# Laying the query and key parts in DRAM by chunk of 512 tokens, and loading a unit's pieces one by one

## The reference

```
xn = layernorm(x)
q, k, v = per head (16 heads of 16 features): xn @ W + b
attention: softmax(causal(q @ k^T / 4)) @ v, heads joined, @ Wo + bo
experts: logits = xn @ Wr; the best 2 of 8 experts, softmax over the two logits
         per expert: (clip(silu(xn @ Wg), -7, 7) * (xn @ Wu)) @ Wd, weighted and added
out = x + attention + experts
```

## Time and profile before

| what | value |
|---|---|
| median of 3 runs | 438.08 us (437.95 to 439.42) |
| the profiled execution | 438.36 us, of which the span of the engines is 436.4 us |
| PE matmul busy | 412.3 us, 94% of the span |
| DVE busy | 332.0 us, 76% |
| ACT, POOL busy | 222.4 us, 196.5 us |
| mean DMA rate | 163 GB/s |

### The profile page before, as it was taken

One profiled execution on the slowest core, in us unless ns is written; L12 is line 12 of the kernel. 1 busy time (PEld: TensorE's weight loads), 2 busy tenths in 40 slices (PEclk: granted clock), 3 DMA queues, 4 the chain that ended last, 5 costly groups with the idle time before them and its releaser, 6 DMA issues.

```text
span 436.4 us, 8151 instructions
## 1 busy us (share of the span) xinstructions
PE 412.3 (94%) x2755; PEld 246.4 (56%) x2755; DVE 332.0 (76%) x1043; ACT 222.4 (51%) x511; POOL 196.5 (45%) x223
## 2 busy tenths in 40 slices
PE   8998979989999999999799999999999999999993
PEld 8585414655364465566547567565667476556332
DVE  6827999999989859775287866789396988881795
ACT  1563362334646566545164355456555445646970
POOL 5331266576064187256474265415655255313320
PEclk9999979999999999999899999999999999999996
DMA  7289896788067089235954239805595336110782
GB/s 228 82 218 194 289 200 211 226 285 282 3 160 174 1 252 279 75 110 170 214 168 156 103 110 249 248 24 182 164 235 178 136 101 194 24 26 6 236 271 72
DMA packets 40372, 71.33 MB, mean 163 GB/s; under 512 B 5893, under 2 KB 30598, under 8 KB 40332
## 3 DMA queue, kind: packets, MB, share of 16 engines
q0 software_dynamic: 9360, 39.99, 29.1%
q1 hardware_dynamic: 27132, 26.76, 25.0%
q10 hardware_dynamic: 3840, 4.08, 3.7%
HBM read 55.85 MB, written 15.60 MB: 164 GB/s over the span
## 4 chain that ended last, share of the span: by engine, by line
PE 68%; DVE 21%; DMA 4%; issue 4%; ACT 1%; POOL 1%; SPq 0%; ACTq 0%; DVEq 0%; POOLq 0%
PE psum L1293 14%; PE psum L1330 14%; PE psum L1254 11%; PE psum L1273 11%; PE psum L1339 8%; DVE psum L981 7%; DVE mxa L984 4%; PE psum L1209 3%; PE psum L1185 3%; PE psum L1312 3%; DMA bqk<-in_bqk 2%; PE psum L1320 2%; DMA xg<-xn_rows,token 2%; DVE resid L953 1%; DMA x<-in_x 1%
## 5 line engine op out<-in xcount | busy, mean ns | idle before, releaser
L894 ACT ACTIVATE probs<-psum 128x512 f32<-128x512 f32 (+1 forms) x320 | 151.1, 581 | 40.9 <-PE psum L1273 40.3
L981 DVE CUSTOM_DVE_ANT_0 psum<-psum,maskrow 128x128 f32<-128x128 f32 (+3 forms) x256 | 121.4, 506 | 14.3 <-PE psum L1254 14.0
L1254 PE MATMUL psum<-packk,packq 96*128 96x512 bf16 (+3 forms) x384 | 94.2, 328 | 3.3 <-DVE mxb L981 1.2
L1273 PE MATMUL psum<-packq,packk 99*128 99x512 bf16 (+3 forms) x384 | 91.0, 330 | 3.3 <-ACT probs L894 2.1
L984 DVE TENSOR_REDUCE mxa<-psum 128x1 f32<-128x512 f32 x128 | 87.7, 685 | 5.4 <-PE psum L1254 5.3
L1293 PE MATMUL psum<-probs,v 128*32 128x512 f32 (+3 forms) x768 | 75.7, 503 | 1.0 <-POOL probs L821 0.9
L1254 PEld LDWEIGHTS psum<-packk,packq 96*128 96x128 bf16 x384 | 35.1, 97 | 56.1 <-issue 15.9
L821 POOL TENSOR_SCALAR_AFFINE_SELECT probs<-probs 128x512 f32<-128x512 f32 (+1 forms) x48 | 41.2, 863 | 44.8 <-ACT probs L894 44.7
L1273 PEld LDWEIGHTS psum<-packq,packk 99*128 99x128 bf16 x384 | 33.4, 98 | 42.7 <-issue 10.5
L788 POOL DMA_INDIRECT xg<-xn_rows,token x39 | 37.7, 967 | 38.9 <-PE psum L1320 27.4
L806 POOL DMA_INDIRECT expert_rows<-wvr,slots x39 | 39.3, 1008 | 31.8 <-ACT wvr L914 17.2
(11 more groups left out here) (120 smaller groups left out, 457.8 us busy)
## 6 DMA issues: line engine op xcount, KB each, us to landing
qk_parts<-stage SPq DMA_DIRECT2D x24, 256.0 KB, 3.9
stage<-expert_rows SPq DMA_DIRECT2D x16, 256.0 KB, 4.1
packq<-qk_parts SPq DMA_DIRECT2D x16, 192.0 KB, 5.4
packk<-qk_parts SPq DMA_DIRECT2D x14, 192.0 KB, 5.8
x<-in_x SPq DMA_DIRECT2D x4, 512.0 KB, 6.2
packq<-qk_parts SPq DMA_DIRECT2D x16, 128.0 KB, 6.0
xn_rows<-probs ACTq DMA_DIRECT2D x4, 512.0 KB, 14.7
out<-x SPq DMA_DIRECT2D x16, 128.0 KB, 3.0
```

Of the source, the lines that this page charges most:

```text
L894: act.activation(probs[:, g % RING, h, 0:width], psum[:, bank, 0:width], ACT.Exp, scale=SCALE)\
L981: ins = dve.tensor_tensor_reduce(out=chunk, in0=chunk, in1=maskrow[:, BANK - width:], scale=1.0, scalar=NEG, op0=ALU.add, op1=ALU.max, acc ...
L1254: pe.matmul(psum[:, bank, 0:width], packq[0:MAXROW, u % SLOTS, i // HALF, h, P * (i % HALF):P * (i % HALF + 1)], packk[0:MAXROW, u % SLOTS ...
L1273: ins = pe.matmul(psum[:, bank, at:at + width], packk[0:KROWS, u % SLOTS, j // HALF, h, P * (j % HALF):P * (j % HALF + 1)], packq[0:KROWS, ...
```

## The change

The DRAM tensor of the parts gets another order of dimensions: the chunk of 512 tokens moves ahead of feature and head. The four heads of one feature and one chunk then lie in one run of 4 x 512 x 2 = 4096 bytes, where before each head had a run of 1024 bytes. The loads are written with the dimensions part, feature, and heads-with-tokens; before, part and feature were one dimension. In the new order of the tensor, the chunk dimension stands between part and feature.

From unit 3 on, each of the six pieces has its own release: piece number c x 3 + r waits for step 10(u - 2) - 1 + (3(c x 3 + r) // 2), which is that same first step and the steps 1, 3, 4, 6 and 7 after it. The planner is given the same condition, so it orders the loads anew. Units 0 to 2 wait for what they waited for before.

```diff
+LOAD_EVERY = 3
...
+def step_before_load(u, c, r):
+
+    return NS * (u - SLOTS + 1) - 1 + (c * len(RUNS) + r) * LOAD_EVERY // 2
...
     for u in range(UNITS):
         b, g = divmod(u, G)
         for c in range(2):
-            after = [("SP", ("store", 4 * b + 2 * (g // 2) + c))]
-            if u >= SLOTS:
-                after += [("PE", ("s", NS * (u - SLOTS + 1) - 1, UH - 1))]
             due = 8 + 10 * c if u == 0 else 60000 + c if u == 1 else nat_due(u, 0) - 30000 + c
             for r in range(len(RUNS)):
+                after = [("SP", ("store", 4 * b + 2 * (g // 2) + c))]
+                if u >= SLOTS:
+                    after += [("PE", ("s", step_before_load(u, c, r), UH - 1))]
...
-        qk_d = nc.dram_tensor("qk_parts", [2, 2, PARTS, HD, H // 2, N], BF16).ap()
+        qk_d = nc.dram_tensor("qk_parts", [2, 2, PARTS, N // BANK, HD, H // 2, BANK], BF16).ap()
...
-                    cols = slice(T * b + BANK * n, T * b + BANK * (n + 1))
-                    sp.dma_start(qk_d[:, grp, part, :, :, cols].rearrange("o d h t -> (d h) o t"),
+                    sp.dma_start(qk_d[:, grp, part, T // BANK * b + n, :, :, :].rearrange("o d h t -> (d h) o t"),
...
-                    wait_filled(sp, ("s", NS * (u - SLOTS + 1) - 1, UH - 1))
+                    wait_filled(sp, ("s", step_before_load(u, c, r), UH - 1))
...
-                    src = qk_d[op, grp, first[op]:first[op] + length, :, h0:h0 + UH, T * b + BANK * c:T * b + BANK * (c + 1)]
-                    sp.dma_start(pack[row:row + HD * length, u % SLOTS, c, :, :],
-                                 src.rearrange("r d h t -> (r d) h t")).then_inc(pack_in[u % SLOTS][c], 16)
+                    src = qk_d[op, grp, first[op]:first[op] + length, T // BANK * b + c, :, h0:h0 + UH, :]
+                    sp.dma_start(pack[row:row + HD * length, u % SLOTS, c, :, :].rearrange("p h t -> p (h t)"),
+                                 src.rearrange("r d h t -> r d (h t)")).then_inc(pack_in[u % SLOTS][c], 16)
...
-              act.dma_start(packk[row:row + HD * length, 0, c, :, :],
-                              qk_d[1, 0, first:first + length, :, 0:UH, BANK * c:BANK * (c + 1)].rearrange("r d h t -> (r d) h t"))\
+              act.dma_start(packk[row:row + HD * length, 0, c, :, :].rearrange("p h t -> p (h t)"),
+                              qk_d[1, 0, first:first + length, c, :, 0:UH, :].rearrange("r d h t -> r d (h t)"))\
```

## The result

The changed kernel takes 478.3 us (median of 4 runs, 475.75 to 480.46) against 438.19 us (437.95 to 439.42) on the same chip: a ratio of 1.0907, 95% interval [1.0849, 1.0964]. That is 18 us above the forecast of 460.4 us and 2.3 us beyond its range.

A forecast was written before the change was run, and what follows sets the result against it. PE was taken as the bound (412.3 of 436.4 us busy), with DVE full from 54 to 110 us. Sum: 438.36 + 23.3 - 2 + 1 = 460.7, median 460.4 us; range 446 to 476 us.

The forecast's parts named there:

- Part 1, the size of a run: Loads: a 4 KB packet takes 163 ns (208 ns for the range), saving 0.6 us per engine and unit.
- Part 2, how many engines: Loads of 3 or 2 parts run on 3 or 2 engines, one-part loads on 16; every transfer starts at the same engine.
- a choice between bounds: Same starting engine gives it 33 packets per chunk and operand; rotating gives even load, cost near nothing; the first was taken.
- rivals A, C and D: A: still 16 engines, 432 us, 0.11; C: three engines rotating, 438 to 441; D: all hidden, 438; C and D 0.07.
- Part 3, the start: Loads of units 0 and 1 fill one engine until 77.2 us; store 2 lands at 79.5; start costs 24.6 - 1.3 = 23.3 us.
- The signs: Profile after: fewer q1 packets, neg 0 near 50 us, first L1273 at 77 us, PE idle about 55 to 77 us.
- As a sign against it: Behind 130 us: PE gaps summing to over 5 us would show the forecast wrong.
- nothing after the start: From unit 3: 21.5 us of packets per unit fit between releases in some 48 us, so the loads cost nothing.
- neg has 4 steps of room: nothing: SP's queue: a load waiting for its step holds up a later neg, which has 4 steps of room; cost nothing.
- The operands are in time: nothing: From unit 3: last piece is released at the unit's seventh step, wanted after the tenth; cost nothing.
- Part 4, burst and gathers: Behind 110 us: of the burst's 4.9 us, 2 come back; other gathers meeting loads on that engine add 1.
- Rival B: Three engines, but worse: 208 ns packets give 473 us, or longer ACT stand gives 480; chance beyond 474 us 0.06.

The follow-up runs named there:

- chunk outside: Changed kernel with DRAM order chunk, part, feature, so part and feature are one dimension again; 4 KB runs and releases one by one kept: 440.46 us, 1.0067.
- part by part: Changed kernel, DRAM order and releases kept, every transfer of two or three parts split into transfers of one part, 16 features outermost: 441.19 us, 1.0065.
- 7.6 by the experiment: Changed kernel with neg 2 placed ahead of unit 3's first piece in SP's order: 470.66 us (3 executions), 1.0746.

## Why the prediction was wrong in size

**Part 1, the size of a run.** The price of a packet held nearly: 0.163 us forecast, 0.184 in the mean and 0.159 mostly in a stretch with little else, and 0.170 over the whole first pile, (81.4 - 28.2 - 6.0 - 2.3) / 264. The small gain came too, as engine time: with 16 engines and the releases one by one, q1's packets took 0.220 x 438.6 x 16 = 1544 us in 4 KB runs (chunk outside) and 0.235 x 436.1 x 16 = 1640 us in 1 KB runs, 0.8 us less per engine and unit (96 / 16 / 7.5, as half of unit 0 goes by q10), forecast 0.6. It did not shorten the kernel: these 4 KB runs cost 4.0 to 5.5 us where I had put nothing. How much of that also lies in the changed kernel's 42 us no run tells.

**Part 2, how many engines.** Right, and shown twice (chunk outside the part, part by part). That all transfers use the same engines was a choice between bounds; the share of 0.22, three packets at a time, decides it, and rivals A, C and D fall.

**Part 3, the start.** The mechanism was right and the term a little small: 26.7 us at the list product against 23.3 (24.6 before the 1.3 us that DVE was to win back behind it). Store 2 was to land at 79.5 us; its chain piece ends at 81.4. The way there was another one than I drew. I had neg 0 and store 2 issued near 50 us and waiting in the queue. In fact SP stood on single issues (5.49, 6.68 us), PE waited 7.7 us for unit 0's own keys, whose landing I had not asked for, and ACT's fourth store of xn stood until 58.7 instead of 49.7 us (its own packets, too, have a share on the busy engines: my reading, not shown). Both waits held PE back, so neg 0 came only at 68.58 us. That the end still came near is partly luck; I take it that one full engine sets it by either way, but no run tests that.

**The signs.** The prediction named q1's packets: 27132 on the page of before, 17682 now, 9450 fewer. That is three quarters of the loads' 11520 packets of 1 KB (8640), and 30 x 13 + 30 x 14 = 810 endings fewer, as 3 and 2 engines in place of 16 give. PE's first L1278 was to come at 77 us and starts at 80.08. Neg 0 near 50 us and PE idle from 55 to 77 us did not come: PE was busy for most of 59 to 75 us. As a sign against it stood "PE gaps behind 130 us that sum to over 5 us", and that came: 3.8 us of idle PE from 165 to 173 us, with a clock of 0.80 and then 0.74 up to 180 us, and 3.3 us at a gather behind 249 us, which the kernel before had too.

**The step that failed: nothing after the start.** The sum stopped at the first pile. Unit 2's twelve loads are another 132 packets, and in SP's order they stand ahead of store 4, as they do in the kernel before. 132 x 0.163 = 21.5 us of engine. The chain shows store 4 landing 16.75 us after its issue, PE waits 5.5 us for a gather beside it, and 8.0 us came through to neg 1. I had used the rule "what stands behind the loads in SP's queue" for neg 0 and store 2 and not again for the next store. The experiment with unit 1's loads later shows how steep this is.

**Part 4, "neg has 4 steps of room: nothing".** Wrong for neg 2, by 6.5 us at the marks (7.6 by the experiment). The planner puts unit 3's first piece one place ahead of neg 2, and the piece waits for the step that ends at 157 us, just when neg 2 is ready and soon wanted. I had checked how long neg could be held by SP's wait, but not how long it then needs on an engine that has 32 packets of 4 KB in front. I priced that pair at 5.2 us alone; with a fetch beside it neg took 12.39 us. "The operands are in time: nothing" did hold.

**Part 4, burst and gathers.** -2 + 1 forecast, about +0.9 found (42.1 less 26.7, 8.0 and 6.5). The reading under it was wrong. I put PE's wait of 3.3 us for a gather behind 204 us, and the low clock after it, down to the twelve loads issued together. Both stay where the loads are spread. The changed kernel has the same 3.3 us at the same gather (the shorter wait of the 8.8 us), in this stretch:

```profile
244.00:260.00 16.00, 12.67 (x90) 10.22 (x87) 3.58 (x11) 3.61 (x10) 8.64 (x10) 0.79 0.50 165
```

And in the old layout with the releases one by one:

```profile
PE psum L1325 <- DMA xg<-xn_rows,token: 2.7, 1, 2.7
```

with a clock of 0.55 and 0.60 from 212 to 216 us. By this pair of profiles the burst had 0.6 of the 3.3 us; what else holds this gather up is open. The release one by one is worth 1.0 us in the old layout, half of what I gave it.

Together: 26.7 + 8.0 + 6.5 + 0.9 = 42.1 us. The forecast had 22.3. The two missing waits are 14.5 of the 19.8 us between, the start 3.4, the rest 1.9.

Rival B's numbers (473 and 480 us) were nearer. Its slow packets of 208 ns did not come in the start (170 ns), and its longer stand of ACT did, by 9 us, but that took part in a start of 26.7 us, not of 35; what makes up the difference lies behind it.

## What to carry to other kernels

When a tensor's order is changed so that runs get longer, look first at what becomes the outermost dimension of each transfer on both sides: chunk, part, feature in place of part, chunk, feature was worth 38 us here, and the longer run nothing good. When a transfer gets slow on one engine, follow every later transfer that is queued behind one like it, up to the last, and ask when each is wanted; one small urgent transfer a single place behind a big pair cost about 7 us. A pile that delays one thing can't be judged by moving it away: price what it will stand in front of next. And before a wait is put down to the transfers issued beside it, spread them and see whether it goes.

## What was unexpected of the hardware

With many packets waiting on few engines, the issuing engine itself stands, for single issues of up to 6.68 us on SP (0.44 before) and 17.11 us on ACT (4.27 before), though 12 or 13 of the 16 engines are idle (share 0.22). An engine that also computes loses all that time: ACT had no copy between 42.4 and 58.7 us.

Loads in 4 KB runs on 16 engines are not clearly faster than in 1 KB runs: one by one, those of 192 KB landed in a median of 3.9 us against 4.3, those of 128 KB in 3.6 against 2.9, and the kernel was 0.9% slower, though its packets took less engine time (part 1 above). Why is open.

No version ran clearly below the kernel before. The nearest is the old layout with the loads one by one, 0.9976 [0.9953, 0.9999].
